# Cross attention: thirteen probability transposes in one run over four PSUM banks, score runs of 4, 4 and 8

## The reference, cut to what matters

```
q = layernorm(x) Wq^T + bq          k = ctx Wk^T + bk          v = ctx Wv^T + bv
scores[b, s, t] = sum_e q[b, s, e] k[b, t, e]
attended = softmax(scores over t) v
x = x + attended
```

## Time and profile before

| | |
|---|---|
| median of 3 runs | 1310.11 us (1308.2 to 1310.57) |
| time of the profiled execution | 1309.42 us |
| its span | 1307.6 us, 63760 instructions |
| busy share of the span: PE, PEld, DVE, ACT, POOL | 94%, 61%, 61%, 34%, 21% |
| mean granted TensorE clock over the span | 0.977 |
| chain that ended last, by engine | PE 81%, DVE 9%, issue 4%, POOL 2%, ACT 1%, DMA 1% |
| HBM traffic | 172.37 MB read, 37.75 MB written |

### The profile page before, as it was taken

One profiled execution on the slowest core, in us unless ns is written; L12 is line 12 of the kernel. 1 busy time (PEld: TensorE's weight loads), 2 busy tenths in 40 slices (PEclk: granted clock), 3 DMA queues, 4 the chain that ended last, 5 costly groups with the idle time before them and its releaser, 6 DMA issues.

```text
span 1307.6 us, 63760 instructions
## 1 busy us (share of the span) xinstructions
PE 1223.3 (94%) x28879; PEld 803.6 (61%) x28879; DVE 802.9 (61%) x1603; ACT 440.8 (34%) x894; POOL 277.3 (21%) x470
## 2 busy tenths in 40 slices
PE   9999999999999999999999999786898989789995
PEld 6864333333333333776667766566787878689995
DVE  5566677777777672465555656364756657357774
ACT  2323211321122112221222212225555537257772
POOL 1100000000000001121222212014352515236663
PEclk9999999999999999999999999899999999989996
DMA  8887999899989992411011110400412203644333
GB/s 296 283 258 231 306 298 307 276 314 299 313 268 319 300 305 65 109 65 64 1 65 64 64 48 0 130 34 34 161 65 96 90 39 154 230 166 113 113 65 65
DMA packets 66133, 211.56 MB, mean 162 GB/s; under 512 B 12240, under 2 KB 28624, under 8 KB 51568
## 3 DMA queue, kind: packets, MB, share of 16 engines
q1 hardware_dynamic: 66032, 210.16, 48.6%
HBM read 172.37 MB, written 37.75 MB: 161 GB/s over the span
## 4 chain that ended last, share of the span: by engine, by line
PE 81%; DVE 9%; issue 4%; POOL 2%; ACT 1%; DMA 1%; SPq 1%; POOLq 0%; DVEq 0%; ACTq 0%
PE ps L714 14%; PE ps L563 10%; PE ps L1087 8%; PE ps L2244 5%; DVE arena L575 5%; PE ps L2276 5%; PE ps L2195 5%; PE ps L235 4%; PE ps L1201 4%; PE ps L1108 4%; PE ps L478 3%; PE ps L2173 2%; PE ps L704 2%; PE ps L2289 2%; PE ps L2230 2%
## 5 line engine op out<-in xcount | busy, mean ns | idle before, releaser
L575 DVE STREAM_TRANSPOSE arena<-arena 128x448 f32<-128x448 f32 (+1 forms) x512 | 263.4, 578 | 98.5 <-PE ps L563 79.5
L563 PE MATMUL ps<-arena 32*64 32x400 f32 (+1 forms) x4096 | 202.8, 506 | 2.6 <-DVE arena L575 1.8
L714 PE MATMUL ps<-arena 128*64 128x512 f32 x832 | 189.2, 598 | 0.0
L563 PEld LDWEIGHTS ps<-arena 32*64 32x64 f32 x4096 | 74.9, 130 | 99.5 <-issue 50.7
L714 PEld LDWEIGHTS ps<-arena 128*64 128x64 f32 x832 | 55.5, 136 | 121.3 <-issue 112.0
L598 ACT ACTIVATE arena<-ps,arena 128x384 f32<-128x384 f32 x64 | 36.3, 582 | 276.4 <-DVE arena L589 276.4
L1087 PE MATMUL ps<-arena 128*128 128x256 f32 x512 | 115.3, 383 | 0.8 <-ACT arena L1022 0.8
L1087 PEld LDWEIGHTS ps<-arena 128*128 128x128 f32 x512 | 97.3, 192 | 17.5 <-issue 3.3
L887 POOL TENSOR_TENSOR arena<-arena 128x1024 f32<-128x1024 f32 x8 | 19.0, 2370 | 405.7 <-PE ps L714 405.7
L2091 ACT COPY arena<-ps 128x512 f32<-128x512 f32 x128 | 75.1, 587 | 75.5 <-PE ps L2244 49.1
L1922 DVE SCALAR_TENSOR_TENSOR arena<-ps,arena 128x512 f32<-128x512 f32 x64 | 69.9, 1117 | 38.3 <-PE ps L2230 37.9
(11 more groups left out here) (161 smaller groups left out, 1895.0 us busy)
## 6 DMA issues: line engine op xcount, KB each, us to landing
arena<-ctx SPq DMA_DIRECT2D x64, 1024.0 KB
arena<-ctx SPq DMA_DIRECT2D x32, 768.0 KB
arena<-q_n SPq DMA_DIRECT2D x64, 256.0 KB, 11.2
h_n<-arena SPq DMA_DIRECT2D x16, 1024.0 KB, 4.4
arena<-h_n SPq DMA_DIRECT2D x16, 1024.0 KB, 7.8
arena<-x SPq DMA_DIRECT2D x16, 512.0 KB, 4.3
arena<-ctx SPq DMA_DIRECT2D x32, 256.0 KB
x_n<-arena SPq DMA_DIRECT2D x16, 512.0 KB, 3.5
```

The costliest lines, as they stand in the source:

```text
L563: last = pe.matmul(ps[b * SEQ:(b + 1) * SEQ, tb, 0:WIDTH[tb]], qs[p % 2][r, db, b * SEQ:(b + 1) * SEQ], z[r, at % RING, b, 0:WIDTH[tb]], s ...
L575: vec.transpose(z[:, at % RING, :, g * 224:g * 224 + nt * 32].rearrange("p b (j t) -> p b j t", t=32), slots[slot_of(k)][:, :, 0:nt, db * ...
L714: last = pe.matmul(ps[b * SEQ:(b + 1) * SEQ, OB, :], probt[:, j, b * SEQ:(b + 1) * SEQ], slot[:, b, jj, :], start=j == 0, stop=j == TILES - 1)
```

## The change

The 13 transposes of a pair now stand in one run ahead of its first score step. The four groups go to four banks: 4, 5, 7 (AB) and 6 (OB). Group 2 first waits until `attended_out` of the pair before last has emptied AB, group 3 until `attended` of the pair before has emptied OB. ScalarE copies the groups out in the order 0, 1, 3, 2; attend 0 waits for the third of these copies, attend 8 for the fourth. The score steps of a loop stand in runs of 4, 4 and 8. In the first loop the wait for the row biases comes ahead of the transposes. After the loop, the last pair's transposes are one run too, and a wait for all copies stands ahead of `transpose_attended(PAIRS - 2)`.

```diff
+    PROB_BANKS = (TB, TB + 1, AB, OB)
+    OUT_ORDER = (0, 1, 3, 2)
...
-            for g in range(4):
+            for g in OUT_ORDER:
                 act.wait_ge(s_pt, 4 * p + g + 1)
                 if p and g == 0:
                     act.wait_ge(s_pv, TILES * p)
                 if g < 3:
-                    act.copy(probt[:, 4 * g:4 * g + 4, :], ps[:, TB + g % 2, :].rearrange("p (j n) -> p j n", j=4))\
-                       .then_inc(s_pte, 1)
+                    act.copy(probt[:, 4 * g:4 * g + 4, :],
+                             ps[:, PROB_BANKS[g], :].rearrange("p (j n) -> p j n", j=4)).then_inc(s_pte, 1)
                 else:
-                    act.copy(probt[:, FULL, :], ps[:, TB + 1, 0:P]).then_inc(s_pte, 1)
+                    act.copy(probt[:, FULL, :], ps[:, PROB_BANKS[g], 0:P]).then_inc(s_pte, 1)
...
-        def transpose_prob(p, g):
-            if g == 0:
-                pe.wait_ge(s_exp, EXPS * (p + 1))
-            n = 4 * p + g
-            if n >= 2:
-                pe.wait_ge(s_pte, n - 1)
-            for j in quarter(g):
-                at = (j - 4 * g) * P
-                last = pe.transpose(ps[:, TB + g % 2, at:at + P], prob[:, j, :, :].rearrange("p b t -> p (b t)"), ident)
-            last.then_inc(s_pt, 1)
+        def transpose_prob(p):
+            pe.wait_ge(s_exp, EXPS * (p + 1))
+            for g in range(4):
+                if g == 2 and p >= 2:
+                    pe.wait_ge(s_ate, p - 1)
+                if g == 3 and p:
+                    pe.wait_ge(s_att, p)
+                for j in quarter(g):
+                    at = (j - 4 * g) * P
+                    last = pe.transpose(ps[:, PROB_BANKS[g], at:at + P],
+                                        prob[:, j, :, :].rearrange("p b t -> p (b t)"), ident)
+                last.then_inc(s_pt, 1)
 
         def attend(p, j):
             if j % 4 == 0:
-                pe.wait_ge(s_pte, 4 * p + j // 4 + 1)
-            if j == 0 and p:
-                pe.wait_ge(s_att, p)
+                pe.wait_ge(s_pte, 4 * p + (3, 3, 4, 4)[j // 4])
...
-                if p == 1 and db == 1:
+                if p == 1 and db == 0:
                     pe.wait_ge(s_re, 2)
-                if db < 4:
-                    transpose_prob(p - 1, db)
+                if db == 0:
+                    transpose_prob(p - 1)
...
-        for g in range(4):
-            transpose_prob(PAIRS - 1, g)
+        transpose_prob(PAIRS - 1)
         pe.wait_ge(early.s_vw, 32)
         pe.wait_ge(early.s_ats, 16)
         for par in range(2):
             for c in range(DC):
                 values(pe, ps, early, par, c)
+        pe.wait_ge(s_pte, 4 * PAIRS)
         transpose_attended(PAIRS - 2)
```

## The result

The changed kernel takes **1294.95 us** (median of 6 runs, 1293.53 to 1301.86) against 1308.88 us for the kernel before (6 runs, 1308.05 to 1310.57, the three shown ahead of the prediction among them). The ratio is 0.9902, 95% interval 0.9878 to 0.9926: 1.0% faster. The forecast was 1297 us, 1293 to 1302.5. The execution profiled took 1294.38 us, 15.0 less than the one of before.

The account below looks back on a forecast made before the run. The prediction took PE's order of work as the bound. 14 x 0.85 + 0.53 + 0.9 = 13.3 us, less 0.6 for late landings, gave 12.7 us: 1309.42 to 1296.7, forecast as 1297 us, range 1293 to 1302.5.

Parts of the forecast that it names:

- The bound: In cross attention's loops PE's own order of work bounds, busy 26.35 of 26.40 us; the DMA queue is next.
- The score run: In each loop, four single score steps taking 3.44 us become one run of 2.87 us, saving 0.57 us.
- The transposes: In each loop, all 13 probability transposes in one run take 1.52 us without a wait, for 1.96 before.
- the wait for bank 6: Before a loop's 13th transpose, PE waits for ACT's L666; the first score step then starts at 261.44, transposes taking 1.68 us.
- the sum: Over cross attention: 14 x 0.85 + 0.53 + 0.9 = 13.3 us saved, less 0.6 for late landings: 12.7 us.
- First and last loop: The first loop saves 0.53 us after an earlier row-bias wait; after the last loop 0.9 us are saved.
- The late context: In the loops, the context's odd half lands 0.85 us later against PE, costing 0.6 us in all (0 to 6).
- The limit: PE loses time only when the context lands 0.55 us or more after a loop's start, a wait over 1.76 us.
- The queue as a bound: Rival: the DMA queue becomes the loops' bound, each saving only 0.4 us, 1302.5 us; chance 0.13.
- The clock: Rival: TensorE's clock falls in the loops' long transpose runs, 13 us slower, 1322 us; chance 0.04.
- The waits for banks 6 and 7: Rival: in the loops these waits eat the saving, 1 us a loop, leaving 1310 us; chance 0.03.

Follow-up runs that it names:

- banks: The changed kernel with its four banks, waits and copy order, but the transposes' four groups back between the score steps: 1306.77 us, ratio 0.9984.
- noq: The changed kernel without the query loads of pairs 2 to 15: 1296.64 us, ratio 0.9910.
- the repeat: The changed kernel run once more with nothing altered: 1294.33 us, ratio 0.9891 to the kernel before.
- moved: The changed kernel with pair p-2's attended transposes ahead of attend 7 to 12 and their ScalarE copies ahead of the exponentials: 1297.33 us, ratio 0.9922.
- r466: The changed kernel with score runs of 4, 6 and 6 steps in place of 4, 4 and 8: 1289.7 us, ratio 0.9868.
- movednoq: The kernel moved without the query loads of pairs 2 to 15: 1294.4 us, one run.

## Why the prediction was right

**The bound** was read rightly: PE's order. *banks* shows that the banks, the waits and the order of the copies give nothing in the loops, *noq* that the queue next to it does not bind.

**The score run.** Forecast 2.87 us for 3.44, from the run of four in the same loop; measured 2.87 to 2.90.

**The transposes.** Forecast 1.52 us without a wait, 1.68 with the wait for bank 6; measured 1.53 and 1.55 in the first two loops (102.80 to 104.33 and 128.19 to 129.74, with no such wait, where the sum had it in the second loop too) and 1.69 in the others. A loop came to 25.59 us where 25.57 was forecast. The price of a change of mode could be read from the kernel before because it held runs of one and of four side by side.

**First and last loop.** Forecast 0.53 and 0.9 us saved; measured 1.01 - 0.55 = 0.46 and 0.97.

**The late context** is the term that was mis-sized: 0.6 us forecast, under 0.1 measured (two first score runs of 2.89 and 2.90), as DVE's waits were 2.21 us in the mean, which was forecast, but the longest was 2.71 and not 2.17 + 0.85 = 3.02 (before they went from 0.67 to 2.17, now from 1.48 to 2.71). The limit was right: 1.76 in waits of before is 2.61 in those of after, a wait of 2.68 cost 0.02 us, and one of 2.86 in the repeat 0.19.

**What no step held:** 0.98 us lost ahead of the loops and 2.8 won behind them. Without them the change's own share is 12.2 + 1.0 = 13.2 us, for 12.7 in the sum; the medians differ by 1308.88 - 1294.95 = 13.9. The prediction had left the second open and had no term for the first. Their net 1.8 us took the total away from the forecast and not towards it (1309.42 - 13.2 = 1296.2 against the forecast of 1296.7), so the range was not met by their luck.

**The rivals.** The queue as a bound fell here with 0.4 us to spare on the context's landing (2.61 against a mean of 2.21), less than the 1.5 us that the prediction read from the mean share. It became true in part in moved and r466, two kernels that go only 0.5 us further; *movednoq* shows the queue as the cause for moved, while for r466 it is read from DVE's waits alone. The Trainium skill ("DMA: Bandwidth & Descriptors", section "Where 436 GB/s comes from") gives 358 GB/s of HBM for a core, by which (22.1 us of transfers a loop, the prediction's estimate from that page) the queue would be no rival in either. As a ceiling the trace disagrees with it: from 248.7 to 252.9 us the kernel before moved 413 GB/s. As a sign of room it disagrees too: first score runs grew in loops with a mean rate of 302 to 309 GB/s. The clock did not fall in runs over twice as long. The waits for banks 6 and 7, which were to eat the gain, came to 0.17 us in 13 loops.

## What to carry to other kernels

Where a loop alternates between matmuls on tiles of the array and full-array transposes, count the changes of mode and price them from the trace: find a run of one and a run of several in the same loop and compare starts. A wait of the weight load can lie inside the time that such a change takes anyway; here removing 21.3 us of such waits alone gained nothing. When the bound engine gets faster, restate every transfer's landing against it: how late the consumer may get the data, how late it gets it now, and from which instruction the load is released. The mean share of the DMA engines (0.91 before, 0.94 after) did not show how near the limit was; the consumer's wait loop by loop did.

## What the runs showed that was not expected

In r466 and moved the queue's lateness comes in alternation (waits of 2.0 and 3.2 us, 1.8 and 3.4, in neighbouring loops): this fits a queue that catches up in the loop that TensorE loses and falls behind in the next, so that mostly every other loop pays. It was not tested.

416 more transposes ahead of them made the unchanged stages behind cross attention slower by 30 and 34 us (813.6 and 818.2 us for 783.9), with longer pauses of PE in their loops and more time at the lower clock. An experiment that adds instructions can so change stages that it does not touch, and has to be read stage by stage.
